# Inverse row sums turned in 32x32 blocks on VectorE and spread over partitions by transfers, in place of TensorE transposes

## What is computed

```
scores = einsum('bhqd,bhkd->bhqk', query, key) * scale
scores = where(causal, scores, -1e9)
attn   = softmax(scores, axis=-1)
out    = einsum('bhqk,bhkd->bhqd', attn, value)     # 16 heads, per batch of 512 tokens
return out @ W_o
```

## Time and profile before

| | |
|---|---|
| runs | 1387.38 us median of 3 (1386.99 to 1387.48) |
| profiled execution, first to last instruction | 1381.9 us, so the runs' median is 5.5 us more |
| granted TensorE clock, mean | 0.981 |
| busy, whole span | PE 1291.0 (93%), PEld 959.9 (69%), ACT 858.4 (62%), DVE 844.4 (61%), POOL 617.0 (45%) |
| chain that ended last | DVE 11%, PE 10%, issue 9% |

### The profile page before, as it was taken

The page is one execution under the profiler, slowest core; times in us unless marked ns, Lnnn a source line. Parts: engine busy times, 40 slices in busy tenths (PEclk is TensorE's granted clock), DMA queues, the critical chain, the costliest instruction groups (busy, mean ns, idle before and its releaser), DMA issues. The chain is left out here.

```text
span 1381.9 us, 24599 instructions
## 1 busy us (share of the span) xinstructions
PE 1291.0 (93%) x7384; PEld 959.9 (69%) x7385; DVE 844.4 (61%) x3207; ACT 858.4 (62%) x2326; POOL 617.0 (45%) x542
## 2 busy tenths in 40 slices
PE   4999769999999999969999999997999999999997
PEld 3666446767777667757788888886667767777765
DVE  4587678777777677723333333333777777777774
ACT  1455427776677577635556656664777777777673
POOL 1111117777775777710000000001888888887820
PEclk9899979999999999999999999998999999999999
DMA  9977653333327422259976666664565665765510
GB/s 342 392 281 275 253 228 114 101 106 111 115 98 256 162 95 92 85 155 316 329 232 188 188 183 190 188 186 126 100 92 87 129 99 90 132 104 89 97 28 31
DMA packets 147284, 223.28 MB, mean 162 GB/s; under 512 B 13846, under 2 KB 128214, under 8 KB 142294
## 3 DMA queue, kind: packets, MB, share of 16 engines
q1 hardware_dynamic: 99350, 157.72, 33.9%
q0 software_dynamic: 36864, 53.50, 18.9%
q10 hardware_dynamic: 10944, 10.49, 2.6%
HBM read 105.27 MB, written 116.39 MB: 160 GB/s over the span
## 5 line engine op out<-in xcount | busy, mean ns | idle before, releaser
L1523 POOL DMA_INDIRECT l_sums<-sorted_y,slot_no x192 | 300.1, 1563 | 424.7 <-DMA l_sums<-base_dram 366.9
L1068 POOL DMA_INDIRECT sorted_x<-f_xn_row,slot_no x192 | 204.7, 1066 | 49.2 <-issue 44.5
L1224 ACT ACTIVATE f_prob<-f_prob,f_negmax 128x512 f32<-128x512 f32 (+3 forms) x256 | 142.6, 557 | 121.3 <-DVE f_negmax L1297 110.8
L2075 DVE SCALAR_TENSOR_TENSOR act_f<-hidden,rows_in,ps 128x96 f32<-128x96 f32 x224 | 70.5, 315 | 231.1 <-ACT hidden L2038 231.0
L1676 ACT ACTIVATE l_prob<-l_prob,l_negmax 128x512 f32<-128x512 f32 (+3 forms) x256 | 141.7, 555 | 104.9 <-DVE l_negmax L1760 97.2
L2000 PE MATMUL ps<-wgu_sb,xt_e 128*128 x896 | 184.2, 328 | 0.5 <-issue 0.4
L1565 PE MATMUL ps<-l_kt,l_qt 128*128 128x512 f32 (+3 forms) x512 | 170.5, 447 | 5.4 <-DVE l_qt L1751 4.8
L1127 PE MATMUL ps<-kt_s,f_qt 128*128 128x512 f32 (+3 forms) x512 | 170.8, 448 | 5.0 <-DVE f_qt L1288 4.4
L1297 DVE CUSTOM_DVE_ANT_0 f_prob<-ps,mask_add 128x512 f32<-128x512 f32 (+3 forms) x256 | 121.0, 486 | 83.5 <-issue 82.5
L1760 DVE CUSTOM_DVE_ANT_0 l_prob<-ps,mask_add 128x512 f32<-128x512 f32 (+3 forms) x256 | 121.0, 486 | 81.0 <-issue 79.7
L2000 PEld LDWEIGHTS ps<-wgu_sb,xt_e 128*128 128x128 f32 x896 | 139.9, 190 | 3.0 <-issue 2.0
(11 more groups left out here) (194 smaller groups left out, 2660.6 us busy)
## 6 DMA issues: line engine op xcount, KB each, us to landing
sorted_x<-zeros SPq DMA_DIRECT2D x14, 2304.0 KB, 9.8
rows_in<-sorted_x SPq DMA_DIRECT2D x112, 288.0 KB, 3.1
sorted_y<-rows_out SPq DMA_DIRECT2D x112, 256.0 KB, 2.1
wgu_sb<-in_wgu SPq DMA_DIRECT2D x16, 384.0 KB, 5.2
x_in<-in_x SPq DMA_DIRECT2D x8, 512.0 KB, 10.3
xn_dram<-xn SPq DMA_DIRECT2D x8, 512.0 KB, 4.0
base_dram<-x_in SPq DMA_DIRECT2D x8, 512.0 KB, 2.9
nqt_dram<-nqt_out SPq DMA_DIRECT2D x8, 512.0 KB, 3.9
```

Of the source, the lines that this page charges most:

```text
L1068: pool.indirect_dma_start(sorted_x, bass.IndirectOffsetOnAxis(ap=slot_no[:, t, k:k + 1], axis=0), xn_row[buf][:], None).then_inc(scattered ...
L1224: act.activation(prob[:, i, qt, 0:w], prob[:, i, qt, 0:w], ACT.Exp, bias=negmax[:, i, qt:qt + 1], scale=-1.0, accum_out=rowsum[:, g // 2 % ...
L1523: pool.indirect_dma_start(sums[n % NSUM][:, t, :], None, sorted_y, bass.IndirectOffsetOnAxis(ap=slot_no[:, TT * GROUPS[n] + t, k:k + 1], a ...
```

## The change

In both heads stages:
- VectorE: `rinv` is 32 columns wide for each parity of the pair (8 used, the rest set to 0 once). After the reciprocal VectorE waits for it and transposes 128x32 in 32x32 blocks into `rinv_t`.
- SyncE: `spread_norms`, in even steps for the pair two steps back, stores `rinv_t` to `norm_dram` (16 KB), waits for the landing, and loads it with two transfers into `norms`, one for each head of the pair, each a row of 512 numbers broadcast to 64 partitions (128 KB). `norms` has two buffers, and `latent_norm` waits for both loads in place of `norms_copied`.
- Removed: `spread` and its copies (GpSimd in the first stage, ScalarE in the last), TensorE's `turn_norms` with its waits, ScalarE's `copy_norms`, and the wait of `queries` for `norms_copied`.
- SyncE's stream becomes `pipeline(step)`: the loads and stores of `during` are issued at fixed steps. The stores of the kept weights and of the rope table go to step 1 of batch 2, the two weight chunks to steps 3 and 5 of it.

```diff
+def spread_norms(sp, done, rinv_t, norms, norm_dram, b, p):
+    n, at = NP_ * b + p, p % 2
+    sp.wait_ge(done.rinv_turned, n + 1)
+    sp.dma_start(norm_dram[at].rearrange("c g q -> g c q"), rinv_t[:, at, :]).then_inc(done.norms_stored, 16)
+    sp.wait_ge(done.norms_stored, 16 * (n + 1))
+    flat = norm_dram[at, 0:2 * TT].rearrange("(i t) g q -> i (t g q)", i=2)
+    for i in range(2):
+        sp.dma_start(norms[i * KVR:(i + 1) * KVR, at, :], flat[i:i + 1, :].to_broadcast([KVR, S]))\
+          .then_inc(done.norms_loaded[i], 16)
...
+            def step(bt, g):
+                if g % 2 == 0 and bt.back(g, 2):
+                    b, h = bt.back(g, 2)
+                    spread_norms(sp, done, rinv_t, norms, norm_dram, b, h // 2)
+                b = bt.now
+                if b + 1 < HB:
+                    if g == 6:
+                        queries_first(b)
+                    if g == 10:
+                        values_first(b)
+                    if g == 14:
+                        queries_second(b)
+                if b > 0:
+                    if g == 0:
+                        residual_base(b - 1)
+                    if g == 2:
+                        values_second(b - 1)
+                    if g == 8:
+                        residual_store(b - 1)
+                if b == 2 and g == 1:
+                    for k in range(2):
+                        sp.dma_start(wq_dram[k], wq_s[k][:].bitcast(F32)).then_inc(kept, 16)
+                        sp.dma_start(wvo_dram[k], wvo_s[k][:].bitcast(F32)).then_inc(kept, 16)
+                    sp.dma_start(rope_dram, rope_t[:]).then_inc(kept, 16)
+                if b == 2 and g in (3, 5):
+                    weights.load_chunk(sp, g // 2 - 1, wgu, wd)
...
-            def spread_inverses(b, p):
-                pool.wait_ge(rinv_ready, NP_ * b + p + 1)
-                pool.tensor_tensor(spread[:, p % 2], rinv[:, p % 2].rearrange("p i t -> p t i").unsqueeze(3)
...
-                if NP_ * b + p > 2:
-                    pe.wait_ge(norms_copied, NP_ * b + p - 2)
...
-            def turn_norms(b, p):
-
-                pe.wait_ge(q_abs, min(NH * b + 2 * p + 6, NH * HB))
-                pe.wait_ge(spread_ready, NP_ * b + p + 1)
-                for t in range(TT):
-                    mm = pe.transpose(norms_ps[:, t * P:(t + 1) * P],
-                                      spread[:, p % 2, t].rearrange("p i n -> p (i n)"), ident[:])
-                mm.then_inc(norms_turned, 1)
...
-            def copy_norms(b, p):
-
-                act.wait_ge(norms_turned, NP_ * b + p + 1)
-                act.wait_ge(lat_normed, NP_ * b + p)
-                act.activation(norms[:], norms_ps, ACT.Copy).then_inc(norms_copied, 1)
...
-                dve.reciprocal(rinv[:, p % 2], rowsum[:, p % 2]).then_inc(rinv_ready, 1)
+                dve.reciprocal(rinv[:, p % 2, 0:2 * TT], rowsum[:, p % 2].rearrange("p i t -> p (i t)"))\
+                   .then_inc(rinv_ready, 1)
+                dve.wait_ge(rinv_ready, NP_ * b + p + 1)
+                dve.transpose(rinv_t[:, p % 2, :], rinv[:, p % 2, :]).then_inc(rinv_turned, 1)
...
-                dve.wait_ge(norms_copied, NP_ * b + p + 1)
-                dve.tensor_tensor(lat[:, p % 2, :], o_ps, norms[:], ALU.mult).then_inc(lat_normed, 1)
+                for i in range(2):
+                    dve.wait_ge(norms_loaded[i], 16 * (NP_ * b + p + 1))
+                dve.tensor_tensor(lat[:, p % 2, :], o_ps, norms[:, p % 2, :], ALU.mult).then_inc(lat_normed, 1)
```

More of the change, by code:

```diff
@@ L86, in build @@
         wvo_dram = dram("wvo_dram", (2, P, NP_, H))
+        norm_dram = dram("norm_dram", (2, SQ, P // SQ, SQ))
         sorted_x = dram("sorted_x", (NTILE * P, HW))
@@ L932, in heads_first @@
     rowsum = sb("f_rowsum", [P, 2, 2, TT])
-    rinv = sb("f_rinv", [P, 2, 2, TT])
-    spread = sb("f_spread", [P, 2, TT, 2, KVR])
+    rinv = sb("f_rinv", [P, 2, SQ])
+    rinv_t = sb("f_rinv_t", [P, 2, SQ])
+    norms = sb("f_norms", [P, 2, S])
     one = sb("f_one", [P, 1])
@@ L1492, in store_out, with queries_first, values_first, queries_second @@
                 sp.dma_start(out_t[b], res[:]).then_inc(res_stored, 16)
-            def during(b):
+            def queries_first(b):
                 sp.wait_ge(q_ready, 2 * (NP_ * b + QUART))
                 sp.dma_start(nqt[0][:].bitcast(F32), nqt_dram[b + 1]).then_inc(nqt_loaded[0], 16)
+            def values_first(b):
                 sp.wait_ge(pv_ready, NP_ * b + QUART)
                 sp.dma_start(nkv[0][:], nkv_dram[b + 1]).then_inc(nkv_loaded[0], 16)
+            def queries_second(b):
                 sp.wait_ge(q_ready, 2 * (NP_ * b + NP_))
                 sp.dma_start(nqt[1][:].bitcast(F32), nqt_dram[b + 1]).then_inc(nqt_loaded[1], 16)
+            def values_second(b):
                 sp.wait_ge(pv_ready, NP_ * b + NP_)
                 sp.dma_start(nkv[1][:], nkv_dram[b + 1]).then_inc(nkv_loaded[1], 16)
-                store_out(b)
-            for b in range(HB, B - 1):
-                during(b)
+            def step(bt, g):
+                if g % 2 == 0 and bt.back(g, 2):
+                    b, h = bt.back(g, 2)
+                    spread_norms(sp, done, rinv_t, norms, norm_dram, b, h // 2)
+                b = bt.now
+                if b + 1 < B:
+                    if g == 6:
+                        queries_first(b)
+                    if g == 10:
+                        values_first(b)
+                    if g == 14:
+                        queries_second(b)
+                if b > HB:
+                    if g == 2:
+                        values_second(b - 1)
+                    if g == 8:
+                        store_out(b - 1)
+            pipeline(step)(sp)
             store_out(B - 1)
```

96 lines of the change are left out of this document (33 added, 63 removed).

## The result

The median went from 1387.18 to 1364.61 us (4 runs each, on one chip; the change's runs are 1362.96 to 1367.82): a ratio of 0.9852, 95% interval 0.9829 to 0.9875, or 22.6 us less. The prediction was 29.2 us less, at 1358. The profiled execution of after took 1365.02 us with a span of 1363.3. Every run of after and of the experiments has 1.7 to 1.8 us between its span and its own time, and the runs of before that stand beside them have 1.7 to 4.4. So the 5.5 us taken as fixed were not a fixed distance: the other 3.8 are partly a larger distance and partly a profiled execution of before that was quicker than its median. The spans differ by 18.6 us, and these 18.6 are what can be laid out place by place.

The account below looks back on a forecast made before the run. TensorE, busy 97% of both heads stages, was taken to bound the kernel. The terms -33.9 + 1.0 + 2.7 + 1.0 = -29.2 us took 1387.4 to 1358 us, range 1347 to 1372.

Parts of the forecast that it names:

- the 5.5 us taken as fixed: Distance from the profiled execution's span, 1381.9 us, up to the median of the runs, assumed unchanged.
- Step 1: Four transposes leave TensorE ahead of `values`: 0.53 us for each of 64 groups, 33.9 us less.
- Step 2: VectorE's transpose (0.2 us) and wait (0.1) make it 0.3 us later in the even step, beside other work.
- The first rival: VectorE takes over part of the gain in every even step: 13 us come back, 1371 us; chance 0.13.
- the wait for `pt`: TensorE's weight loads or `values` waiting for copies of `pt` in every pair would show the first rival.
- Step 3: ScalarE's copy of the turned probabilities delays `values` by 0.03 us in 32 first-stage pairs: 1.0 us more.
- Step 4: Norms' store and loads take 5.3 us, with 3.1 us spare in every pair, and cost nothing.
- The slower rival: Transfers late in every pair of the last stage: 48 us more, 1406 us; chance 0.10.
- Step 5: SyncE's queue: norms behind the burst in batch 2 are 5.2 us late once; net 2.7 us more.
- the bound: Upper bound on the burst's net cost, +8 us, if the scatter's rows are late as well.
- Step 6: At the stage ends nothing covers the transfers: 1.0 us more in the last stage, nothing in the first.
- The third rival: TensorE is not the limit at `values`, which starts unchanged: 1384 to 1388 us; chance 0.07.

Follow-up runs that it names:

- Experiment 1: Kernel before the change without its turning of norms: no copies, transposes or transfers, norms set to ones once; 1360.29 us, ratio 0.9826.
- experiment 6: Changed kernel with GpSimd's `lat_lo` put two scatters later in the first stage; 1371.68 us, ratio 0.9897.
- experiment 4: Changed kernel with VectorE's transpose of the inverses done twice, first into a buffer nobody reads; 1367.09 us, ratio 0.988.
- experiment 2: Changed kernel with VectorE's reciprocal and transpose moved behind the maxima of piece 1; 1364.66 us, ratio 0.9859.
- experiment 7: Changed kernel with the store of the norms done twice, one after the other, before the loads; 1374.37 us, ratio 0.9914.
- experiment 5: Changed kernel without the norms' store and loads, norms set to ones, burst kept at step 1; 1361.84 us, ratio 0.9829.
- experiment 9: Changed kernel with the burst split and, in the first stage, ScalarE's `latent_hi` ahead of the exponentials of piece 1; 1363.39 us, ratio 0.984.
- experiment 10: Kernel of experiment 9 plus filler transposes of the identity on TensorE at both heads stages' ends; 1360.63 us, ratio 0.9817.
- experiment 11: Changed kernel with the burst split, plus filler transposes of the identity at both stage ends; 1358.5 us, ratio 0.9791.

## Why the prediction was right, and where it was off

The direction, the mechanism and the range held: 1364.6 lies in 1347 to 1372. The point was 6.6 us too low on the median. With 22.6 us less against 29.2, it is a size that was off. By its own steps:

**Step 1 failed in its size.** The 0.53 us were read from the start of the first transpose to the start of `values`, and I wrote that `values` "can follow them at once". The four products cost 0.44; 0.09 is a distance that stays in front of `values`. Over 64 groups that is 5.8 us. Experiment 1, where nothing replaces the transposes, gives the same pair. In the first stage up to 0.11 us a pair more, 2.4 us by the difference of the two stages, goes to the exclusion of VectorE and GpSimd (experiment 6), which the prediction didn't have. By the distances between `latent_norm`, 60 pairs gave 23.0 us and the stretch up to the first one 2.3, against 33.9.

**Step 2 held**: 0.21 and 0.25 us against 0.2 and 0.3, hidden, as experiments 1 and 4 show. The first rival, VectorE taking over, did not come in: the wait for `pt` that it named as its sign is there without the change's work as well (experiment 1). But it was nearer than it looked, since 0.14 us more on VectorE show by half. **Step 3**: the 1.0 us for ScalarE's copy wasn't paid. The copy ends at 301.42 and `values` starts at 301.54, where the distance behind the scores sets it anyway (experiment 2).

**Step 4 held for the result, with less to spare.** First stage, but for the burst: 5.4 to 7.1 us of chain, at least 2.2 spare ahead of the last pair, against 5.3 and 3.1. Last stage: 5.5 to 8.8 us, 0.1 to 1.3 spare in eight pairs. The load takes 3.0 and 3.5 us to land against 2.6, the two loads are issued 0.51 apart against 0.3, and from the store to the loads it is up to 3.3 against 2.1 + 0.1. The slower rival was nearer than its 0.10 said, but experiment 7 shows that its price was wrong: a norm that is late before a piece step is made good in that step, so not 1.5 us a pair, and 2 us in every chain made the time 9.8 us longer and not 48.

**Step 5 held in mechanism and in net**: one wait, at the step named, 6.2 us against 5.2, and the store held for 10.8 us behind the burst against 10.9; net +3.4 against +2.7. Both gross sizes were larger (7.7 against 5.2 after, 4.3 against 2.5 before), because the scatter's rows on ScalarE's queue are late too, which I had put only into the bound.

**Step 6 was too small**: the last pair of each stage and the stretch behind the last one cost 3.8 us more (0.6, 1.7, 1.5) against 1.0. The chain itself is longer than forecast, 6.04 to 6.30 us from the reciprocal where 5.8 was put. The clock wasn't costed at all: without the transposes TensorE idles 0.90 us before the last `values` instead of 0.46, in after the granted clock is at 0.50 in both of them, and of the 1.5 us behind the last `latent_norm` 1.1 are there without transfers too (experiments 1 and 5) and none with filler (13.7 us, as before). The waits for the norms that were forecast at the ends don't show in after, as `values` ended 0.2 to 0.5 us later than the second load. **The third rival** (no gain at that place) is out.

**The sum** would then be -25.3 (pairs and start) + 3.4 + 3.8 - 0.5 (between the stages) = -18.6, the difference of the spans. The 22.6 of the medians is larger by the 3.8 us of before's 5.5 that were no fixed distance. That the medians come nearer to the forecast than the spans do is luck: laid out by place, the two profiled executions differ by 18.6 of the 29.2.

## What to carry to other kernels

Price an instruction that leaves a stream by the distance of its neighbours' starts (0.109 us each, 0.44 for four), not by the distance to whatever comes next, since part of that stays. A small transfer that an engine waits for must not share a queue with a burst: cutting 4.5 MB into pieces between the small ones, with the weight chunks moved as well, gave 7.2 us, a third of what the change itself gave. At a stage's end nothing hides a longer chain, and products that look like a cost can be worth their place by the clock that they keep: read the granted clock before and after there, and at more than one end, since it fell in the last `values` at 10 ends of 22.

## What was not expected of the hardware

- An operation of VectorE with two SBUF inputs and one of GpSimd exclude each other: 0.69 us became 0.80, 1.49 and 1.82 by how much they met (after, experiments 9 and 6), and VectorE's always ended 0.54 to 0.56 us after GpSimd's.
- The granted clock was 0.50 in the last `values` of after, and 16 products took 4.06 us instead of 2.37. With the same 0.90 us of idle time it happened at 10 stage ends of 22; before has two ends, and it happened at neither, which is too few to show that the four transposes prevented it. Transposes of the identity as filler held the clock at 1.00 at all four ends, to the end of the last stage (experiments 10 and 11).
- One 16 KB packet that loads instructions, 0.95 us long, made the last sixteenth of a 128 KB load land 1.1 us late (experiment 11).
- Two transposes of 128x32 on VectorE, one behind the other, start 0.14 us apart, although each is shown as 0.17 to 0.21 us.
- The issue of the store takes SyncE 0.56 us and of a load 0.50, against 0.32 for the load in the earlier trace rows. That load itself takes 0.59 in after. So it is not the kind of transfer; what in the new stream of SyncE lengthens it, no run tells.
